# One core of a fused attention and routed-FFN layer: queries of two tiles projected as [feature, token], tile 4's routing inside the loop, a new queue order ahead of it, final layers in column halves

## The reference, cut to what matters

```python
h = concat([gather(x, curve) @ proj_w.T + proj_b, txt], axis=1)   # (4, 768, 192)
# attention, 6 heads, on n = layernorm(h)
Q, K = xpos(n @ Wq, +1), xpos(n @ Wk, -1)      # heads of 128: [x1 c - x2 s, x1 s + x2 c]
V, gate = n @ Wv, silu(n @ Wg)                 # heads of 64
out = (Q @ K.T * 128**-0.5 * decay_mask) @ V   # causal, decaying, row-normalised
h = h + (groupnorm(out) * gate) @ Wo
# routed FFN on m = layernorm(h): 8 groups s, rank 16, 64 experts of width 32, 4 chosen
z = einsum('nd,sdr->nsr', m, P)
topv, topi = top_k(einsum('nsr,smr->nsm', z, C), 4)
w = softmax(topv)
y = sum_k w_k * (gelu(z @ W1[s, topi_k] + b1) @ W2[s, topi_k] + b2)
h = h + gelu(y.reshape(n, 128) @ G1 + g1b) @ G2 + g2b
```

## Time and profile before

| | us |
|---|---|
| median of 3 runs | 920.6 (918.74 to 922.23) |
| profiled execution, its own time | 925.56 |
| its span, first to last instruction | 923.7 |
| PE busy | 879.9 (95%) |
| DVE busy | 663.0 (72%) |
| ACT busy | 567.5 (61%) |
| POOL busy | 474.4 (51%) |

### The profile page before, as it was taken

The page is one execution under the profiler, slowest core; times in us unless marked ns, Lnnn a source line. Parts: engine busy times, 40 slices in busy tenths (PEclk is TensorE's granted clock), DMA queues, the critical chain, the costliest instruction groups (busy, mean ns, idle before and its releaser), DMA issues.

```text
span 923.7 us, 16126 instructions
## 1 busy us (share of the span) xinstructions
PE 879.9 (95%) x5422; PEld 399.8 (43%) x5422; DVE 663.0 (72%) x1657; ACT 567.5 (61%) x844; POOL 474.4 (51%) x445
## 2 busy tenths in 40 slices
PE   8899999999999988899799999999999999999997
PEld 3477777777678766222222222222232223222222
DVE  6566555665667577677687888788878887877774
ACT  1121211225332354688788798889988897988784
POOL 0335343333335523476756666757575756574452
PEclk8999999999999999699999999999999999999999
DMA  9600002000000096768687888888988888889773
GB/s 246 230 1 1 2 1 74 1 1 1 1 1 16 15 143 159 188 209 267 181 245 229 254 246 268 242 267 236 295 226 270 247 278 224 276 252 290 243 251 100
DMA packets 89805, 154.14 MB, mean 167 GB/s; under 512 B 30212, under 2 KB 56069, under 8 KB 89330
## 3 DMA queue, kind: packets, MB, share of 16 engines
q1 hardware_dynamic: 89236, 151.48, 54.9%
q10 hardware_dynamic: 486, 1.62, 1.2%
HBM read 138.81 MB, written 15.83 MB: 167 GB/s over the span
## 4 chain that ended last, share of the span: by engine, by line
PE 75%; ACT 8%; DMA 5%; DVE 5%; issue 3%; POOL 2%; SPq 1%; ACTq 0%; DVEq 0%; POOLq 0%
PE ps L854 16%; PE ps L791 15%; PE ps L495 9%; PE ps L503 5%; PE ps L830 5%; PE ps L568 4%; PE ps L560 3%; PE ps L577 3%; DMA w_parts<-wp 2%; ACT ring L1168 2%; PE ps L538 2%; DMA wbc<-w_rows 1%; PE ps L590 1%; PE ps L621 1%; PE ps L642 1%
## 5 line engine op out<-in xcount | busy, mean ns | idle before, releaser
L1829 POOL TENSOR_TENSOR ring<-ring,wbc 128x512 f32<-128x512 f32 x192 | 245.0, 1278 | 160.5 <-ACT ring L1179 147.6
L1628 DVE TENSOR_TENSOR ring<-ps,ring 128x1024 f32<-128x1024 f32 x192 | 234.6, 1222 | 85.8 <-PE ps L830 57.1
L791 PE MATMUL ps<-zst,w1st 99*128 99x512 bf16 x768 | 213.9, 389 | 14.7 <-ACT ring L1168 7.2
L854 PE MATMUL ps<-ring,w2cur 128*32 128x512 f32 x1536 | 205.8, 609 | 0.0
L1168 ACT ACTIVATE ring<-ps 128x1024 f32<-128x1024 f32 x192 | 196.7, 1025 | 4.2 <-PE ps L791 4.1
L1690 POOL TENSOR_TENSOR t<-t 128x768 f32<-128x768 f32 x48 | 87.5, 1834 | 189.7 <-DVE t L1310 189.7
L1181 ACT ACTIVATE ps<-ps 128x512 f32<-128x512 f32 x192 | 113.2, 589 | 61.2 <-PE ps L791 60.7
L1631 DVE TENSOR_TENSOR ring<-ps,wbc 128x512 f32<-128x512 f32 x192 | 130.8, 682 | 1.6 <-DMA wbc<-w_rows 1.5
L1308 DVE TENSOR_TENSOR t<-ps,rope 128x768 f32<-128x768 f32 x48 | 45.7, 953 | 107.1 <-PE ps L503 70.5
L791 PEld LDWEIGHTS ps<-zst,w1st 99*128 99x128 bf16 x768 | 60.9, 98 | 140.8 <-issue 38.3
L1179 ACT ACTIVATE ring<-ps 128x512 f32<-128x512 f32 x192 | 116.3, 606 | 0.0
(11 more groups left out here) (173 smaller groups left out, 1121.4 us busy)
## 6 DMA issues: line engine op xcount, KB each, us to landing
wbc<-w_rows SPq DMA_DIRECT2D x192, 512.0 KB, 5.3
w2cur<-in_w SPq DMA_DIRECT2D x48, 256.0 KB, 4.4
w_parts<-wp SPq DMA_DIRECT2D x72, 64.0 KB, 3.1
zst<-z_parts SPq DMA_DIRECT2D x72, 64.0 KB, 4.7
wst<-w_parts SPq DMA_DIRECT2D x24, 128.0 KB, 3.9
z_parts<-zp SPq DMA_DIRECT2D x6, 384.0 KB, 5.3
wst<-w_parts SPq DMA_DIRECT2D x24, 96.0 KB, 3.7
out_h<-h SPq DMA_DIRECT2D x12, 192.0 KB, 5.0
```

Source lines behind the costliest of these rows:

```text
L791: return pe.matmul(bank(to), w1st[0:99, 4 * a + j, col:col + P], zst[0:99, (i // 2) % 2, j, :], start=True, stop=True)
L854: mm = pe.matmul(bank(YBANK, 0, 512, 32 * j, 32 * j + 32), w2cur[:, n, j, :], ring[:, (4 * g + j) % RING, :], start=False, stop=(n == 7 an ...
L1628: dve.tensor_tensor(v, ps[:, WBANK * 512:WBANK * 512 + 1024], v, ALU.mult).then_inc(s["duo_done"], 1)
L1829: pool.tensor_tensor(ring[:, slot, :], ring[:, slot, :], wbc[:, g % 4, 1, :], ALU.mult).then_inc(s["tri_done"], 1)
```

## The change

**Queries.** They are projected with the weights stationary and the tokens of both tiles moving (256 columns for a head), so they come out as [feature, token] and need no transpose. Three heads of both tiles stand in PSUM columns 0 to 767, the other three in 1280 to 2047. `rotate_queries` on DVE makes only the product with the cosines (768 columns, per half); the exchange of the feature halves is a copy between partitions on ACT (`swap`, two copies of 64 x 768 per half), whose product with the sines POOL makes (`swapped_queries`) before it adds (`rotated_queries`). `turn` and `keep` keep the keys alone. `xn_turn` transposes 4 pieces (the 64-row parts of each tile on both partition halves).

**Order.** Tile 4's exponential, gates and stores leave the bridge and join tile 5's in iterations 0 and 1, in the order that the later pairs of tiles have. The last output projections use four PSUM banks instead of two. In SP's queue tile 2's stores stand ahead of the second half of W1, and z's and the gates' loads ahead of the first three `spread`. A second z buffer, `zp2`, takes block 2.

**Final layers.** `first_final` puts the two halves of a block's 512 columns on partitions 0 to 63 and 64 to 127, `final_gelu` covers 128 x 256, and the bias g2b is added to h by POOL (`add_bias`).

```diff
...
+            store_rows(2)
+            store_gates(2)
             sp.wait_ge(s["st_w1"], 96)
             sp.wait_ge(s["g_full"], PAIRS)
             sp.wait_ge(s["aq"], TILES)
             sp.wait_ge(s["ak"], TILES)
             load_w1(sp, 1)
-            store_rows(2)
-            store_gates(2)
...
             store_rows(3)
             store_gates(3)
-            for g in range(3):
-                spread(g)
...
             sp.wait_ge(s["zeroed"], 16)
             load_gates(0)
+            for g in range(3):
+                spread(g)
+            store_z(1)
             store_z(2)
-            store_rows(4)
-            store_gates(4)
+            sp.dma_start(g2b[:, :], t["g2"][GH:GH + 1, :].to_broadcast([P, D])).then_inc(s["ld_bias"], 16)
...
-                if i == 0 and n == 7:
-                    store_rows(LEAD)
-                if i == 1 and n == 0:
-                    store_gates(LEAD)
-                if i % 2 == 0 and 0 < i and n == 7 and tile < TILES:
+                if i % 2 == 0 and n == 7 and tile < TILES:
                     store_rows(tile - 1)
-                if i % 2 == 1 and 1 < i and tile <= TILES:
+                if i % 2 == 1 and tile <= TILES:
                     if n == 0:
                         store_gates(tile - 2)
                     if n == 1:
...
-            def queries(k, x):
+            def query_block(e):
+
+                return e // 3 * 1280 + e % 3 * 2 * P
+
+            def queries(k, half):
                 pe.wait_ge(s["xn_e"], k + 1)
                 if k > 0:
-                    pe.wait_ge(s["g_out" if x else "v_out"], 2 * k)
-                whole(2 * x, k, x, 0, QK)
+                    pe.wait_ge(s["g_out" if half else "v_out"], 2 * k)
+                for e in range(3 * half, 3 * half + 3):
+                    at = query_block(e)
+                    pe.matmul(ps[:, at:at + 2 * P], wcat[:, 0, e * P:e * P + P],
+                              xnT[:, k % 2, 0:2, :].rearrange("p x n -> p (x n)"),
+                              start=(at % 512 == 0 or e == 3), stop=False, skip_group_check=True)
+
+            def query_rests(k):
+
+                for n in range(3):
+                    for half in range(2):
+                        e = 3 * half + n
+                        at = query_block(e)
+                        mm = pe.matmul(ps[:, at:at + 2 * P], wcat[D2 * half:D2 * half + D2, 1, e * P:e * P + P],
+                                       xnT[D2 * half:D2 * half + D2, k % 2, 2:4, :].rearrange("p x n -> p (x n)"),
+                                       start=False, stop=True, skip_group_check=True)
+                mm.then_inc(s["q_full"], 1)
...
             def keys(k):
                 if k == 0:
                     pe.wait_ge(s["ld_k"], 16 * 3)
                 for x in range(2):
-                    pe.wait_ge(s["rq"], 2 * k + x + 1)
+                    if x == 0:
+                        pe.wait_ge(s["rq"], 2 * k + 2)
+                    else:
+                        pe.wait_ge(s["sq"], 2 * k + 2)
                     whole(2 * x, k, x, QK, QK)
                 rest(0, 2, k, QK, QK).then_inc(s["k_full"], 1)
...
             def turn(k, x):
-                pe.wait_ge(s["aq"], 2 * k + x + 1)
                 pe.wait_ge(s["ak"], 2 * k + x + 1)
                 if x == 0 and k > 0:
                     pe.wait_ge(s["o_out"], 2 * k)
                     pe.wait_ge(s["st_out"], sums_before(k))
                 if x == 1:
                     pe.wait_ge(s["kept"], 2 * k + 1)
-                for kind in range(2):
-                    for e in range(H):
-                        col = 4 * 512 + (kind * H + e) * P
-                        mm = pe.transpose(ps[:, col:col + P], t1[:, 2 * x + kind, e, :], ident[:, :])
-                mm.then_inc(s["turned"], 1)
-
...
             wo_pair(7, 5)
+            pe.wait_ge(s["x2_e"], 6)
+            wo_pair(8, 2)
+            project_z(2, 7)
+            wo_pair(9, 3)
             pe.wait_ge(s["res"], 7)
-            wo_pair(8, 4)
-            project_z(2, 7)
+            wo_pair(10, 4)
             pe.wait_ge(s["res"], 8)
-            wo_pair(9, 5)
-            pe.wait_ge(s["res"], 9)
-            wo_pair(10, 4)
-            pe.wait_ge(s["res"], 10)
             wo_pair(11, 5)
             pe.wait_ge(s["z_e"], 3)
-            turn_gates(4, 7)
+            pe.wait_ge(s["res"], 10)
+            keep_clock(2)
...
                 for a in range(2):
-                    mm = pe.matmul(bank(to, 0, 512, 0, GH), g1[:, a, :], ysum[:, (2 * blk + a) % 4, :],
-                                   start=(a == 0), stop=(a == 1))
+                    for half in range(2):
+                        mm = pe.matmul(bank(to, 0, 2 * P, GH * half, GH * half + GH), g1[:, a, :],
+                                       ysum[:, (2 * blk + a) % 4, half * 2 * P:half * 2 * P + 2 * P],
+                                       start=(a == 0), stop=(a == 1), skip_group_check=True)
...
+                col = 4 * 512 + x * QK
+                act.copy(kT[:, x, :, :].rearrange("p h n -> p (h n)"), ps[:, col:col + QK]).then_inc(s["kept"], 1)
+
+            def swap(k, x):
+
+                hd = DQK // 2
+                src = ps[:, 1280 * x:1280 * x + QK].rearrange("p (h n) -> p h n", n=P)
+                act.wait_ge(s["q_full"], k + 1)
+                if x == 1:
+                    act.wait_ge(s["rq"], 2 * k + 1)
+                if k > 0:
+                    act.wait_ge(s["aq"], 2 * (k - 1) + x + 1)
+                act.copy(s2q[0:hd, x, :, :], src[hd:P, :, :])
+                act.copy(s2q[hd:P, x, :, :], src[0:hd, :, :]).then_inc(s["sq"], 1)
...
+                swap(k, 0)
+                swap(k, 1)
...
+            def rotate_queries(k, x):
+
+                c = k % CH
+                src = ps[:, 1280 * x:1280 * x + QK].rearrange("p (h n) -> p h n", n=P)
+                dve.wait_ge(s["q_full"], k + 1)
+                if x == 0:
+                    dve.wait_ge(s["sq"], 2 * k + 1)
+                if k == 2 and x == 1:
+                    dve.wait_ge(s["ld_rope1"], 16)
+                if k > 0:
+                    dve.wait_ge(s["aq"], 2 * (k - 1) + x + 1)
+                dve.tensor_tensor(t1q[:, x, :, :], src, _mid(rope[:, c, 0, :], H), ALU.mult).then_inc(s["rq"], 1)
+
+            def rotate_keys(k, x):
...
+            residual(8, 2)
             mark(4, 0, S)
-            residual(8, 4)
-            chosen_exps(4)
-            normaliser(4)
+            residual(9, 3)
             row_stats(6)
+            residual(10, 4)
             row_stats(7)
-            residual(9, 5)
+            residual(11, 5)
             row_stats(8)
-            residual(10, 4)
             row_stats(9)
...
+            def swapped_queries(k, x):
+
+                pool.wait_ge(s["sq"], 2 * k + x + 1)
+                if k == 0 and x == 0:
+                    pool.wait_ge(s["ld_rope0"], 16)
+                if k == 2 and x == 0:
+                    pool.wait_ge(s["ld_rope1"], 16)
+                pool.tensor_tensor(s2q[:, x, :, :], s2q[:, x, :, :], _mid(rope[:, k % CH, 1, :], H),
+                                   ALU.mult).then_inc(s["mq"], 1)
+
+            def rotated_queries(k, x):
+
+                pool.wait_ge(s["rq"], 2 * k + 2)
+                pool.wait_ge(s["mq"], 2 * k + 2)
+                if k > 0:
+                    pool.wait_ge(s["at_full"], 2 * k)
+                pool.tensor_tensor(qT[:, x, :, :].rearrange("p h n -> p (h n)"),
+                                   t1q[:, x, :, :].rearrange("p h n -> p (h n)"),
+                                   s2q[:, x, :, :].rearrange("p h n -> p (h n)"), ALU.add).then_inc(s["aq"], 1)
...
-                rotated(k, 0, 1)
+                rotated_keys(k, 0)
...
+                    weights(1)
+                rotated_queries(k, 0)
+                rotated_queries(k, 1)
...
             distances(4)
-            weights(4)
             z_rest(2)
             z_low(2)
-            high_part(4)
-            low_parts(4)
...
                     distances(tile)
+                if i == 4 and n == 0:
+                    pool.wait_ge(s["ld_bias"], 16)
+                    pool.wait_ge(s["x2_d"], PAIRS)
+                if i % 4 == 0 and i > 0 and n in (1, 2):
+                    add_bias(i // 4 - 1, n - 1)
+                if i == NIT - 3 and n in (1, 2):
+                    add_bias(NBLK - 1, n - 1)
                 if i < 3 and n in (5, 6):
                     x2_make(2 * i + 1 + n)
-                if i == 0:
-                    if n == 3:
-                        weights(tile)
-                    if n == 6:
-                        high_part(tile)
-                    if n == 7:
-                        low_parts(tile)
-                if i % 2 == 0 and 0 < i and tile < TILES:
+                if i % 2 == 0 and tile < TILES:
                     if n == 3:
                         weights(tile - 1)
                     if n == 6:
@@ -1846,7 +1902,7 @@
```

182 lines of the change are left out of this document (86 added, 96 removed).

## The result

The changed kernel takes 906.0 us (median of 4, 905.14 to 906.53), 0.984 of the kernel before, with a 95% interval of 0.982 to 0.986. Timed again in 6 executions it took 904.3 us, a ratio of 0.983 (0.979 to 0.986). Forecast were 901 us; the range of 893 to 910 holds it. Its profiled execution is one of 905.14 us with a span of 903.3, against 925.56 and 923.7 before: the two profiles stand 20.4 us apart, the medians 15 to 16.

The account below looks back on a forecast made before the run. PE was taken to bound attention (282.3 of 283.0 us busy), less so the bridge. Terms -13 - 7.3 + 6.8 - 6.0 = -19.5 us gave 906.1 from the profiled 925.6, hence 901 for the median, range 893 to 910.

Parts of the forecast that it names:

- The step to the median: Whole kernel: profiled execution is 5.0 us above the median of 920.6, so 906.1 by profile becomes 901 us.
- Attention: Attention pairs: PE loses 11 transposes an iteration, -14.2 us over eleven; cuts and waits add 1.2, so -13 us.
- the forecast of its cover: Keys in attention: PE's heads (2.79 us) just cover DVE's second query product (2.6 to 2.7), by about 0.1 us.
- The rule of the Trainium skill: Query cuts: some 60 cycles per matmul would cost 0.2 us an iteration, 2.2 in all, forecast 903; set aside.
- Bridge: Attention's end to the loop: earlier stores and z's load, four banks, no tile 4 exponential; -7.3 us, bounds 3 and 9.
- tile 4's exponential, which leaves: Bridge's end: PE's 3.54 us wait before the last output projections, as DVE waited 3.94 for this exponential, goes.
- Iterations 0 and 1: Loop's start: they take over the late weights of iterations 2 and 3, +6.2, and a second exponential, 0.6: +6.8 us.
- Final layers: Final layers: column halves side by side save 0.9 us in each of five blocks, plus end and memset: -6.0 us.
- (a): Attention: ACT's copies between partition halves run at half rate, keys wait, +23 us, 924; chance 0.06.
- (c): Iteration 0: POOL is in time, or full clock returns; 6 us less, 895; chance 0.12.
- (d): Attention: the queries' 64-row parts no longer run side by side, 14.3 us more in all, 915; chance 0.05.
- (b): Bridge: W1's second half, issued 11 us later, holds up tile 3's stores and later loads; 6 us lost, 907; chance 0.15.

Follow-up runs that it names:

- before_again: The kernel before, unchanged, run again for a second profile: 920.9 us, ratio 1.001.
- before_queue: Kernel before with tile 2's stores ahead of W1's second half and the three broadcasts behind z's and the gates' loads: 915.6 us, 0.994.
- small_waits: tile4_bridge with iteration 2's second weights earlier, keep_clock(2) deleted, and group-norm activations, first x2_out and tile 5's largest moved earlier: 893.4 us, 0.970.
- swap_extra: Changed kernel with one more copy between partition halves in the first swap of each attention iteration: 912.9 us, 0.993.
- tile4_bridge: Changed kernel with tile 4's exponential, gates and stores back ahead of the loop, queue order and banks kept: 898.3 us, 0.977.
- weights_first: Changed kernel with the second tile's weights in iterations 0 and 2 ahead of the x2_make of the same group: 897.1 us, 0.975.

## Why the prediction was nearly right

**The sum against the profile** was right within 1 us, -19.5 forecast and -20.4 measured, in part by luck: attention gave 3.3 us less than forecast in its row, and all other rows together 4 more (1.8 of the last row's 7.5 stand between the two profiles of the kernel before). **The step to the median failed**, and the miss at the median (904.3 to 906.0 us against 901) comes from it. It read "That execution is 5.0 us above the median of 920.6, so for the median I forecast 901 us": it took the 5 us off both kernels alike. before_again shows that most of them stand in the bridge, and before_queue that the new queue takes 5.3 us off the median of the kernel before. A gain read from a slow execution's stall is not had in the executions that have no such stall. From the last heads to DVE's first product the changed kernel is 7.7 us shorter than the first profile of the kernel before and 1.2 us shorter than the second (36.9 against 38.1).

**Attention** was mis-sized: -13 forecast by the eleven pairs, -10.8 measured at the last heads where the forecast had -14.1. Of the 10.8, 0.7 lie ahead of the first pair's heads (50.0 and 49.3 us), where starts scatter by 2 us without any edit. A pair gains 1.16 us, not 1.3: the two turns shrank by 1.3 (2.8 to 1.5), where 12 times 0.117 is 1.4, and `xn_turn` and the cuts cost 0.1 together. In pairs 8 and 9 next to nothing was gained (0.0 and 0.1 us):

```profile
...
PE ps L643 <- DVE oT_a L1447: 1.0, 1, 1.0
...
PE ps L652 <- ACT x2T L1050: 0.8, 1, 0.8
...
```

The second wait was foreseen (0.7), the first was not: the first group norm's twelve activations stand behind four swaps of 0.80 us on ACT, so DVE's gated product comes 1 us late for `wo_pair(0)`. small_waits, which moves both pieces of ACT's work ahead, gets 1.1 us back in each pair. A third wait stands in the last pair and is in no forecast:

```profile
...
319.59 0.66 PE L670 MATMUL ps<-ident,wn 128*128 128x128 f32 x4 [1.01 <-POOL wn L1784]
...
```

It costs nothing that the profile shows, since PE waits 0.60 us more for ACT's `keep` behind it. swap_extra confirms that keys follow DVE's second product; the forecast of its cover, 0.1 us, was 0.05.

The rule of the Trainium skill, "TensorEngine Tiling (Array Packing)", Instruction Overhead, that was set against the cuts: the queries' 12 passes of 256 take 162.53 - 159.94 = 2.59 us here, as the 8 of 512 and 256 columns took before (2.58 in the same place), and the 64-row part 1.57 us against 1.56. With the weight loads hidden, four passes more cost 0.01 us in this trace, where the rule gives, as an estimate at the prediction's 25 ns, 0.1; here the measurement decides.

**Bridge.** Right in the queue's mechanism and in the landing of z (no wait; the last issue at 353.0). The first layer, named for 355, came at 357.70, as attention had ended 3.3 us later than forecast. Wrong in the bridge's second half: "tile 4's exponential, which leaves" as the source of 3.5 us. One DMA wait of POOL caused both rows, through `distances(4)` queued behind the cast; tile 4 itself costs 0.5 us there (tile4_bridge).

**Iterations 0 and 1.** Right in mechanism and size: +5.7 for +6.8, of which the interval at the second turn_gates makes 4.0 and the second exponential 0.6 (4.43 for 3.87); the other 1.2 are in the first intervals of iteration 1 (4.06 for 2.50 at the first). weights_first shows that POOL's order is the cause of the 4.0, so this was a loss that the change did not need; the first intervals of iteration 1 stay long there.

**Final layers.** -6.0 forecast, -6.5 measured alone.

Added up, from medians except where said: queue -5.3 (from the kernel before), attention -10.8 (by the profiles), final layers -6.5, banks and DVE's order -2.7, the added keep_clock +1.7 (by the profiles), tile 4 in the loop +6.0: -17.6 against the 15 to 16 measured. The 2 us left lie within what several such differences can be off by.

**The rivals.** (a) was 0.05 us away (swap_extra), (c) did not come: POOL was late as in iteration 2, though PE's wait was 2.27 us and not 3. (d) is out: the 64-row parts take 1.57 us. (b), a loss by W1's later half, did not come either; what made the bridge's gain small in the median was the other thing, that most executions of the kernel before did not stall there as long as the profiled one.

## What to carry to other kernels

When a profile stands above its kernel's median, find out where before taking terms from it: a wait in it that other executions do not have is a gain that they cannot give. Take a second profile when the spread is wider than the terms. The length of a wait is not its price either: look for what else the instruction would have waited for (7.89 us of wait for a store cost 0.33). When two engines wait in one place, follow both queues back to the first instruction that stood still: here one cast behind a store delayed the parts that z's loads queue behind, and the exponential, too. And when routing work is moved under a loop, move each instruction to where its consumer asks, not to where the pattern of later iterations has it: one `weights` behind two `x2_make` cost some 4 us each time.
